# A relation layer on one core: the vector engine's steps put in another order

## The reference, cut to what matters

```python
# N = 6250 nodes, E = 200000 edges sorted by dst, 32 relations, 8 bases, 128 features
hsrc = h[src]                                # E x 128
coef = w_comp[etype]                         # E x 8
msg = 0
for b in range(8):
    msg = msg + hsrc @ weight[b] * coef[:, b][:, None]
msg = msg * norm                             # norm: E x 1
node_repr = relu(segment_sum(msg, dst, num_segments=N) + bias)
x = layernorm(x + node_repr)                 # h is this x
```

## Time and profile before

| What | Value |
|---|---|
| Runs | 3788.11, 3792.09, 3780.69 us (median 3788.11) |
| The profiled execution | 3789.68 us, span 3787.9 us |
| PE, DVE, POOL, ACT busy, whole span | 3315.4 (88%), 2466.3 (65%), 2442.2 (64%), 1361.5 (36%) us |
| Relation layer, first to last tile addition | 2147.4 to 3764.7 us |
| Chain that ended last | PE 33%, DVE 21%, ACT 18%, DMA 11%, issue 9%, DVEq 7% |

### The profile page before, as it was taken

One profiled execution on the slowest core, in us unless ns is written; L12 is line 12 of the kernel. 1 busy time (PEld: TensorE's weight loads), 2 busy tenths in 40 slices (PEclk: granted clock), 3 DMA queues, 4 the chain that ended last, 5 costly groups with the idle time before them and its releaser, 6 DMA issues.

```text
span 3787.9 us, 52562 instructions
## 1 busy us (share of the span) xinstructions
PE 3315.4 (88%) x16935; PEld 2226.6 (59%) x17077; DVE 2466.3 (65%) x4684; ACT 1361.5 (36%) x3452; POOL 2442.2 (64%) x2636
## 2 busy tenths in 40 slices
PE   3999999998999898999999788878888889798886
PEld 3889999995543333543344455556555666565564
DVE  7999999996686565101203476667666676666675
ACT  5999999992000000000101332223222322232221
POOL 5888888881016666445541477767776767676774
PEclk6999999999999999999999899999999989899997
DMA  6677677778879999999999323323322323232322
GB/s 180 192 206 206 204 209 207 208 205 278 269 230 250 248 236 257 268 266 261 275 266 302 92 74 73 76 68 76 75 76 66 77 70 78 69 73 68 79 66 52
DMA packets 532789, 618.45 MB, mean 163 GB/s; under 512 B 74011, under 2 KB 460127, under 8 KB 532399
## 3 DMA queue, kind: packets, MB, share of 16 engines
q1 hardware_dynamic: 478895, 528.52, 49.6%
q0 software_dynamic: 53616, 86.51, 9.4%
HBM read 445.83 MB, written 168.99 MB: 162 GB/s over the span
## 4 chain that ended last, share of the span: by engine, by line
PE 33%; DVE 21%; ACT 18%; DMA 11%; issue 9%; DVEq 7%; POOL 1%; SPq 0%; POOLq 0%; ACTq 0%
PE PS L1230 19%; ACT arena L844 11%; DMA arena<-adjacency 10%; ACT arena L860 6%; DVE XT L1775 5%; DVEq L1759 5%; DVE H L1755 5%; PE PS L1282 3%; PE PS L1325 2%; DVE arena L1784 2%; PE PS L1308 2%; PE PS L1344 2%; PE PS L1118 2%; DVEq L1775 1%; DVE arena L1734 1%
## 5 line engine op out<-in xcount | busy, mean ns | idle before, releaser
L796 POOL DMA_INDIRECT arena<-x_table,rec x1140 | 1185.1, 1040 | 458.2 <-issue 329.7
L775 POOL DMA_INDIRECT sorted_records<-arena x428 | 505.8, 1182 | 603.3 <-PE PS L1230 516.6
L1118 PE MATMUL PS<-arena 128*98 128x128 f32 x6272 | 761.6, 279 | 46.6 <-DVE arena L1514 13.0
L1118 PEld LDWEIGHTS PS<-arena 128*98 128x98 f32 x6272 | 708.1, 166 | 96.5 <-issue 50.8
L732 POOL TENSOR_SCALAR arena<-iota,H,arena 128x98 f32<-128x98 f32 x980 | 675.4, 705 | 91.0 <-PE PS L1118 88.3
L1230 PE MATMUL PS<-arena,X 128*128 128x512 f32 (+1 forms) x1274 | 545.0, 577 | 59.6 <-DMA arena<-adjacency 59.4
L844 ACT ACTIVATE arena<-arena 128x98 f32<-128x98 f32 x1568 | 583.2, 687 | 12.7 <-DVE arena L1512 12.6
L1230 PE MATMUL PS<-arena,H 128*128 128x512 f32 (+1 forms) x1274 | 535.5, 575 | 31.2 <-DMA arena<-adjacency 30.9
L860 ACT ACTIVATE arena<-PS 98x1024 f32<-98x1024 f32 x392 | 520.2, 1327 | 12.3 <-PE PS L1118 12.3
L1775 DVE TENSOR_TENSOR XT<-XT,PS 128x64 f32 x1140 | 252.0, 221 | 407.8 <-issue 137.0
L1282 PE MATMUL PS<-H,X 128*128 128x512 bf16 x1447 | 461.6, 395 | 62.4 <-DVE H L1755 52.6
(11 more groups left out here) (259 smaller groups left out, 2901.7 us busy)
## 6 DMA issues: line engine op xcount, KB each, us to landing
arena<-adjacency SPq DMA_DIRECT2D x294, 768.0 KB, 8.4
adjacency<-arena SPq DMA_DIRECT2D x196, 784.0 KB
arena<-adjacency SPq DMA_DIRECT2D x98, 832.0 KB, 6.5
arena<-x_table,rec POOLq DMA_INDIRECT x1140
XT<-sorted_source_rows SPq DMA_DIRECT2D x112, 128.0 KB
arena<-in_edge_type SPq DMA_DIRECT2D x226, 48.0 KB
arena<-in_edge_type SPq DMA_DIRECT2D x226, 32.0 KB
XT<-sorted_relations SPq DMA_DIRECT2D x448, 8.0 KB
```

Of the source, the lines that this page charges most:

```text
L775: pool.indirect_dma_start(rec2_d, bass.IndirectOffsetOnAxis(ap=SLOT[:, t:t + 1], axis=0), R4[:, t, :], None).then_inc(s_scat, 16)
L796: pool.indirect_dma_start(G[:, n % HELD_UNITS * UNIT_TILES + i, :], None, x1_d, bass.IndirectOffsetOnAxis(ap=SRC[:, t:t + 1], axis=0)).the ...
L1118: last = nc.tensor.matmul(bank(2 * q + j // 4, P, j % 4 * P)[0:M1, :], S1[:, r, :], S2[:, r, :], start=True, stop=True)
```

## The change

Nothing is computed otherwise. On DVE, `matrix`, `wide_matrix` and `sources` are cut into single steps, and the single steps are placed between the additions that wait for each other:

- place marks and scales stand behind the first and the second tile addition of a step;
- wide marks, matrix part 0, wide scales, matrix part 1 follow in turn;
- one-hots stand between wide additions 0 and 1, between 2 and 3, and behind the first of the late tile additions; four of them alternate with the four parts of the wide product;
- the wide product is made tile by tile (336 columns each), and PE's wide sum c waits for part c alone;
- the three register loads stand before the late tile additions instead of behind them.

PE's, POOL's and SyncE's programs keep their order; only the counts on `s_c2` change.

```diff
--- before.py
+++ after.py
@@ -450,7 +450,10 @@
         s_apart = sem("relations_apart")
         s_coef = sem("coefficients_multiplied")
         s_coefc = sem("coefficients_copied")
+        s_marked = sem("places_marked")
         s_place = sem("places_scaled")
+        s_marked2 = sem("wide_places_marked")
+        s_place2 = sem("wide_places_scaled")
         s_c = sem("matrix_made")
         s_gath = [sem(f"nodes_gathered{j}") for j in range(HELD_UNITS)]
         s_u = sem("basis_sums_made")
@@ -983,7 +986,7 @@
                 act.wait_ge(s_coef, s + 1)
                 if s >= 2:
                     act.wait_ge(s_c, 2 * (s - 1))
-                    act.wait_ge(s_c2, groups_to(s - 2))
+                    act.wait_ge(s_c2, PER * groups_to(s - 2))
                 n = (STEP_TILES + (PER if s < GROUPS else 0)) * BASES
                 nc.scalar.activation(COEF[s % 2][:, 0:n], bank(7, n), ACT.Copy).then_inc(s_coefc, 1)
 
@@ -1321,7 +1324,7 @@
                 n = UNIT[i, "wide", c]
                 unit_bank_free(n)
                 pe.wait_ge(s_turned, i + 1)
-                pe.wait_ge(s_c2, i + 1)
+                pe.wait_ge(s_c2, PER * i + c + 1)
                 nc.tensor.matmul(bank(UNIT_BANKS[n % RING_BANKS], WIDE_BASIS), G2[i % 2][:, c, :], C2[i % 2][:, c, :, :].rearrange("p b j -> p (b j)"),
                                  start=True, stop=True).then_inc(s_u, 1)
 
@@ -1719,41 +1722,54 @@
             def of_step(t, s):
                 return t[:, REGION + s * STEP_TILES:REGION + (s + 1) * STEP_TILES]
 
-            def matrix(s):
+            def places_marked(s):
                 if s:
                     dve.wait_ge(s_c, 2 * s)
-                link(nc.vector.tensor_tensor(PLACE, numbers(STEP_TILES, SPAN), spread(of_step(LOC, s), STEP_TILES, SPAN), ALU.is_equal))
+                nc.vector.tensor_tensor(PLACE, numbers(STEP_TILES, SPAN), spread(of_step(LOC, s), STEP_TILES, SPAN), ALU.is_equal).then_inc(s_marked, 1)
+
+            def places_scaled(s):
+                dve.wait_ge(s_marked, s + 1)
                 nc.vector.tensor_tensor(PLACE, PLACE, spread(of_step(NORM, s), STEP_TILES, SPAN), ALU.mult).then_inc(s_place, 1)
-                dve.wait_ge(s_place, s + 1)
-                dve.wait_ge(s_coefc, s + 1)
+
+            def matrix(s, i):
+                if i == 0:
+                    dve.wait_ge(s_place, s + 1)
+                    dve.wait_ge(s_coefc, s + 1)
+                    if s >= 2:
+                        dve.wait_ge(s_u, UNIT[s - 2, "tile", 1] + 1)
+                first, end = PARTS_OF_STEP[i]
+                ks, n = slice(first, end), end - first
                 coef = COEF[s % 2][:, 0:STEP_TILES * BASES].rearrange("p (t b) -> p t b", b=BASES)
-                if s >= 2:
-                    dve.wait_ge(s_u, UNIT[s - 2, "tile", 1] + 1)
-                for first, end in PARTS_OF_STEP:
-                    ks, n = slice(first, end), end - first
-                    nc.vector.tensor_tensor(C[s % 2][:, ks, :, :], coef[:, ks, :].unsqueeze(3).to_broadcast([P, n, BASES, SPAN]),
-                                            PLACE[:, ks, :].unsqueeze(2).to_broadcast([P, n, BASES, SPAN]), ALU.mult).then_inc(s_c, 1)
-
-            def wide_matrix(i):
-                q = group_of(i)
+                nc.vector.tensor_tensor(C[s % 2][:, ks, :, :], coef[:, ks, :].unsqueeze(3).to_broadcast([P, n, BASES, SPAN]),
+                                        PLACE[:, ks, :].unsqueeze(2).to_broadcast([P, n, BASES, SPAN]), ALU.mult).then_inc(s_c, 1)
+
+            def wide_marked(i):
                 if i:
-                    dve.wait_ge(s_c2, i)
-                link(nc.vector.tensor_tensor(PLACE2, numbers(PER, WIDE), spread(LOC2[:, q, :], PER, WIDE), ALU.is_equal))
-                link(nc.vector.tensor_tensor(PLACE2, PLACE2, spread(NORM2[:, q, :], PER, WIDE), ALU.mult))
-                if i >= 2:
-                    dve.wait_ge(s_u, UNIT[i - 2, "wide", PER - 1] + 1)
-                dve.wait_ge(s_coefc, i + 1)
-                coef = COEF[i % 2][:, STEP_TILES * BASES:(STEP_TILES + PER) * BASES].rearrange("p (t b) -> p t b", b=BASES)
-                nc.vector.tensor_tensor(C2[i % 2], coef.unsqueeze(3).to_broadcast([P, PER, BASES, WIDE]),
-                                        PLACE2.unsqueeze(2).to_broadcast([P, PER, BASES, WIDE]), ALU.mult).then_inc(s_c2, 1)
-
-            def sources(i):
-                dve.wait_ge(s_srow[i % 2], 16 * (i // 2 + 1))
-                if i >= 2:
-                    dve.wait_ge(s_gs, i - 1)
-                for k in range(CLASS_BLOCKS):
-                    last = nc.vector.tensor_scalar(ST2[i % 2][:, k, :], SROW[i % 2], NODE[:, k:k + 1], None, ALU.is_equal)
-                last.then_inc(s_st2, 1)
+                    dve.wait_ge(s_c2, PER * i)
+                nc.vector.tensor_tensor(PLACE2, numbers(PER, WIDE), spread(LOC2[:, group_of(i), :], PER, WIDE), ALU.is_equal).then_inc(s_marked2, 1)
+
+            def wide_scaled(i):
+                dve.wait_ge(s_marked2, i + 1)
+                nc.vector.tensor_tensor(PLACE2, PLACE2, spread(NORM2[:, group_of(i), :], PER, WIDE), ALU.mult).then_inc(s_place2, 1)
+
+            def wide_matrix(i, c):
+                if c == 0:
+                    dve.wait_ge(s_place2, i + 1)
+                    if i >= 2:
+                        dve.wait_ge(s_u, UNIT[i - 2, "wide", PER - 1] + 1)
+                    dve.wait_ge(s_coefc, i + 1)
+                coef = COEF[i % 2][:, (STEP_TILES + c) * BASES:(STEP_TILES + c + 1) * BASES]
+                nc.vector.tensor_tensor(C2[i % 2][:, c, :, :], coef.unsqueeze(2).to_broadcast([P, BASES, WIDE]),
+                                        PLACE2[:, c, :].unsqueeze(1).to_broadcast([P, BASES, WIDE]), ALU.mult).then_inc(s_c2, 1)
+
+            def sources(i, k):
+                if k == 0:
+                    dve.wait_ge(s_srow[i % 2], 16 * (i // 2 + 1))
+                    if i >= 2:
+                        dve.wait_ge(s_gs, i - 1)
+                last = nc.vector.tensor_scalar(ST2[i % 2][:, k, :], SROW[i % 2], NODE[:, k:k + 1], None, ALU.is_equal)
+                if k == CLASS_BLOCKS - 1:
+                    last.then_inc(s_st2, 1)
 
             def heads_loaded(values):
                 return nc.values_load_multi_w_load_instructions(
@@ -1830,31 +1846,55 @@
 
             dve.wait_ge(s_ln, len(CHUNKS))
             dve.wait_ge(s_node, 2 * len(CHUNKS))
-            sources(0)
-            matrix(0)
-            wide_matrix(0)
-            sources(1)
-            sources(2)
+            for k in range(CLASS_BLOCKS):
+                sources(0, k)
+            places_marked(0)
+            wide_marked(0)
+            places_scaled(0)
+            wide_scaled(0)
+            for i in range(2):
+                matrix(0, i)
+            for c in range(PER):
+                wide_matrix(0, c)
+            for i in (1, 2):
+                for k in range(CLASS_BLOCKS):
+                    sources(i, k)
             dve.wait_ge(s_zero, 2)
             first, wide, rest = tile_heads(0, 0), wide_heads(0), tile_heads(0, 1)
             for s in range(OUT_AT[-1] + 3):
                 if KEPT_CHUNK + s < len(CHUNKS):
                     split(KEPT_CHUNK + s)
+                further = s + 1 < STEPS
+                grouped, marking = s + 1 < GROUPS, s + 3 < GROUPS
                 if s < STEPS:
                     for j, base in enumerate(first):
                         tile_added(s, 0, j, base)
-                if s + 1 < STEPS:
-                    matrix(s + 1)
+                        if j == 0 and further:
+                            places_marked(s + 1)
+                        if j == 1 and further:
+                            places_scaled(s + 1)
+                if grouped:
+                    wide_marked(s + 1)
+                if further:
+                    matrix(s + 1, 0)
+                if grouped:
+                    wide_scaled(s + 1)
+                if further:
+                    matrix(s + 1, 1)
                 for m in range(len(OUT_ORDER)):
                     if OUT_AT[m] == s - 1:
                         summed(m)
                 if s < GROUPS:
                     wide_added(s, 0, wide[0])
+                if marking:
+                    sources(s + 3, 0)
+                if s < GROUPS:
                     wide_added(s, 1, wide[1])
-                if s + 3 < GROUPS:
-                    sources(s + 3)
-                if s + 1 < GROUPS:
-                    wide_matrix(s + 1)
+                for c in range(PER):
+                    if marking:
+                        sources(s + 3, c + 1)
+                    if grouped:
+                        wide_matrix(s + 1, c)
                 for n in events_in(s - 1):
                     if consumed(n) == "joined":
                         joined(n)
@@ -1865,16 +1905,23 @@
                     freed = events_to(s - 1, reused)
                     if freed:
```

(19 more changed lines are left out.)

## The result

The changed kernel took 3658.9 us (median of four runs, 3657.4 to 3671.1) against 3784.4 us for the kernel before (four runs, 3779.7 to 3792.1): a ratio of 0.9674, interval 0.9646 to 0.9701, 125 us less. The forecast was 3684, the range 3638 to 3738. In the changed kernel, lines are numbered anew: the tile additions are L1791, the wide ones L1800, the one-hots L1770, the wide product L1762, marks and scales L1728 and L1732 (wide: L1749 and L1753), the loads L1775, the gathers L799; on PE the sources are L1285, the wide sums L1328, the block product L1347; ACT's clearing of a ring buffer is L1028.

The account below looks back on a forecast made before the run. DVE's own order was taken to bound the relation layer's step. Six terms save 1.35 us a step, 151 us over 112 steps; less 47 us given back, 104 us, giving 3684 us, range 3638 to 3738.

Parts of the forecast that it names:

- Terms 1, 3 and 4: DVE's step: place marks and scales between tile additions save 0.54 us; one-hots between wide additions 0.53, behind late tile addition 0.21.
- Term 2: DVE's step: wide marks and scales, set apart from each other, cost 0.25 us in place of 0.72; saves 0.22.
- Term 5: DVE's step: the wide product in four parts of 336 elements costs 0.22 us more than in one piece.
- Term 6: DVE's step: register loads behind a wide addition save 0.28 us, the step's first addition costs 0.21; net 0.07.
- What the new order makes late: Relation layer: the last one-hot comes late for PE; low clock, double block products and late type rows give back 47 us.
- whole saving (below 3660): Rival: DVE's saving arrives whole because PE's clock holds, 3643 us; chance 0.20.
- The clock's part: PE's idle time in one piece halves its clock in every second step with a block product, costing 33 us.
- PEclk below 0.94: Sign: PE's mean granted clock in the relation layer's stage falls below its earlier 0.94.
- the stretching: POOL's gathers last longer under the long wide product, 109 us in all; most of it was expected to go.
- POOL at 3734: Rival: half the gathers' 109 us of stretching and all POOL's waits for PE remain, 3734 us; chance 0.22 (with one-hots).
- The slower case: Rival: late one-hots drop PE's clock in every step and their loop to the loads becomes the bound, 3855 us; chance 0.05.

Follow-up runs that it names:

- the run with the parts alone: The kernel before with the wide product in four parts one behind another, PE's wide sum c waiting for part c alone: 4124.2 us, ratio 1.0153.
- The run with both edits: The changed kernel with the last one-hot ahead of the register loads and DVE waiting for ring buffers by ring: 3602.1 us, ratio 0.9590.

## Why the prediction was right, and where it was not

**The bound.** DVE's own order set the step, as said: the layer fell with it and nothing else did. This rests on the rows of the two profiles; on a chip with prompt updates no part of the change ran by itself.

**The sum of the terms** was 1.35 us a step and is about 1.4. Terms 1, 3 and 4 came as forecast to some hundredths (rows above); the one-hots alone between other forms cost 0.26 to 0.30 us, not 0.33 or 0.41. Term 2: the wide mark and the wide scale cost 0.24 us each, 0.49 in place of 0.72, so 0.23 saved against 0.22. Term 5 cost 0.20 against 0.22; the run with the parts alone shows it without the rest of the change. As an estimate, the fixed cost of small tiles that the Trainium skill names (VectorE: DVE Perf Modes, the TRN2 errata) gave 0.18 for three more instructions; the trace agrees, with 0.20. Term 6 came as forecast: the idle time behind the loads fell from 2.21 and 2.79 us to 1.93 and 2.52, so by 0.28 and 0.27, and the first addition of a step now stands idle for 0.20 (forecast 0.28 and 0.21).

**The step that failed is "What the new order makes late".** It was to give back 47 us; 151 - 125.6 is 25. So 3684 was 25 us high, and 3658.9 falls 1 us into the next of the prediction's own bins, "whole saving (below 3660)", which had a chance of 0.20, not into the likeliest. That the whole came so near is in part luck: the sum of the terms was right by its rows, but what is given back was put nearly twice too high, and by a path that did not come. The clock's part had the right cause, a wrong sum and a wrong way to DVE. PE's idle time in one piece did bring stretches at half clock, behind waits like the 1.97 us one. But "PEclk below 0.94" was wrong: the mean stayed at 0.94 and the low stretches fell from 196 to 158 us, while PE's busy share of the stage rose from 0.84 (1369.90 of 1630) to 0.88 (1329.90 of 1510). The cost did not come as PE's sums too late for DVE's next additions either, but by a path that the prediction doesn't have: block product, ACT's clearing of the ring buffer, and DVE's wait for it ahead of the third wide addition. All DVE waits before wide additions went from 22 to 52 us (those over 250 ns), and these 30 us are about the 25 given back, within what the rows tell. The run with both edits on the chip with prompt updates supports the path by taking most of it away: the waits for the clearing fell by 28 us and the layer by 32. How much the low clock, and how much the mere lateness of the one-hot, made the block product late stays open.

**POOL** was named second with 1406 us and the stretching, with 1517 available. That it is second is right. The mean fell to 988 ns as forecast ("below 990"), but 51 us of stretching remained, and the distance was 50 us, not 111 less the rest. The shorter gathers were more than a sign: 1515 us of busy and issue time, as before, would not have fitted into the 1504 that POOL took. The page SBUF — State Buffer of the Trainium skill, section on who interferes with whom, infers that a DVE instruction with two SBUF inputs doesn't stop descriptor generation. The trace disagrees again: only kernels with the product in one piece have gathers over 1600 ns. The gather also reads its row numbers from SBUF (`SRC`, in `rec`), so it may be this read that is held; no run tells the two apart.

**The rivals.** The whole saving (3643) did not come in this order, but would nearly have; POOL at 3734 did not come. The slower case had the right place, the late one-hots, and the wrong price: the fall of the clock is not in every step. On the chips with late updates the change was slower by some 1 to 2%, by a cause that I had not thought of; of the slower case's mechanism this is no confirmation.

## What to carry to other kernels

Fill the holes between dependent instructions with independent ones of any form, and read each hole from the spacings in one step: here such a sum held to 0.05 us a step. Then follow what the new order makes late to its end, through every engine that clears or frees a buffer, and let a queue wait for the one buffer that its next instruction writes. Before speeding up the bounding engine, sum busy and issue time of the second one: here that floor, 1454 us, was the same in three kernels and told how much there was left to win. Register loads cost next to nothing here with queued work behind them (6 us of idle time in the layer), and 1.9 to 2.8 us a step where the next instruction needs them. And measure on more than one chip before you call a reordering a gain.
